# Decoder layer on one core: the output product moved ahead of u's turns, the projections to the end of the slot before

## The reference, cut to what matters

```python
x = _layernorm(x + self_attention(x))          # softmax(q k^T / sqrt(8)) v, then wo, with biases
x = _layernorm(x + cross_attention(ctx, x))    # k and v from ctx, q from x
x = _layernorm(x + ffn(x))                     # qlinear -> gelu -> qlinear
```

## Time and profile before

| what | us |
|---|---|
| median of 3 runs (lowest, highest) | 355.75 (355.57, 357.69) |
| the profiled execution's own time | 355.31 |
| its span in the profile | 353.5 |
| DVE, PE, ACT, POOL busy | 314.0, 265.0, 252.5, 187.0 |

### The profile page before, as it was taken

One profiled execution on the slowest core, in us unless ns is written; L12 is line 12 of the kernel. 1 busy time (PEld: TensorE's weight loads), 2 busy tenths in 40 slices (PEclk: granted clock), 3 DMA queues, 4 the chain that ended last, 5 costly groups with the idle time before them and its releaser, 6 DMA issues.

```text
span 353.5 us, 13237 instructions
## 1 busy us (share of the span) xinstructions
PE 265.0 (75%) x4897; PEld 171.0 (48%) x4899; DVE 314.0 (89%) x720; ACT 252.5 (71%) x502; POOL 187.0 (53%) x382
## 2 busy tenths in 40 slices
PE   3678887989989999999899988898883365102980
PEld 2446564656656666666665655555551122001660
DVE  5756799989999999999999999999889599997894
ACT  2135877988889888888888887887762599605855
POOL 6234869656675666657675667665222006400275
PEclk9999999999999999999999999999995578755797
DMA  1352323233332332323323242332000000000034
GB/s 52 89 159 69 99 80 88 63 108 90 97 107 74 107 104 84 101 84 102 106 83 107 79 124 84 96 94 71 5 3 0 0 0 0 0 0 3 1 90 149
DMA packets 48998, 25.19 MB, mean 71 GB/s; under 512 B 6440, under 2 KB 48808, under 8 KB 48936
## 3 DMA queue, kind: packets, MB, share of 16 engines
q1 hardware_dynamic: 46936, 23.76, 23.4%
q10 hardware_dynamic: 2000, 0.59, 0.7%
HBM read 9.39 MB, written 2.10 MB: 32 GB/s over the span
## 4 chain that ended last, share of the span: by engine, by line
DVE 32%; PE 30%; POOL 14%; issue 13%; DMA 4%; ACT 3%; SPq 2%; ACTq 0%; POOLq 0%; DVEq 0%; another core or an unknown queue 0%
DVE neg_max L850 14%; PE ps L1083 8%; PE ps L1109 7%; DVE h_ext L957 5%; DVE h_ext L958 5%; DMA arena_h<-parts_sk 4%; POOL rstd L531 3%; PE ps L1167 2%; PE ps L1156 2%; SPq L399 2%; PE ps L1124 2%; PE ps L1144 2%; PE ps L1131 2%; PE ps L1251 1%; POOL o_root L598 1%
## 5 line engine op out<-in xcount | busy, mean ns | idle before, releaser
L850 DVE TENSOR_REDUCE neg_max<-ps 128x8 f32<-128x1024 f32 x128 | 157.2, 1228 | 18.5 <-PE ps L1083 16.0
L652 ACT ACTIVATE probs<-ps 128x1024 f32<-128x1024 f32 x64 | 65.6, 1025 | 19.7 <-PE ps L1090 18.2
L1083 PE MATMUL ps<-arena_h 31*128 31x128 f16 x1024 | 52.8, 221 | 27.3 <-DVE neg_max L850 17.9
L663 ACT ACTIVATE probs<-ps 128x1024 f32<-128x1024 f32 x64 | 65.7, 1026 | 8.5 <-PE ps L1090 8.5
L1083 PEld LDWEIGHTS ps<-arena_h 31*128 31x128 f16 x1024 | 31.0, 94 | 59.9 <-DVE neg_max L850 35.6
L1090 PE MATMUL ps<-arena_h 32*128 32x128 f16 x1024 | 51.7, 219 | 0.6 <-ACT probs L652 0.5
L528 POOL TENSOR_TENSOR var_eps<-mean_var,eps_col 128x1 f32<-128x1 f32 x64 | 12.2, 191 | 73.4 <-DVE mean_var L833 73.4
L1109 PE MATMUL ps<-probs,arena_q 128*32 128x128 f32 x1024 | 42.1, 283 | 0.9 <-issue 0.9
L1109 PE MATMUL ps<-probs,arena_h 128*32 128x128 f32 x1024 | 41.6, 281 | 0.2 <-ACT probs L652 0.2
L531 POOL TENSOR_TENSOR rstd<-var_eps,minus_half 128x1 f32<-128x1 f32 x64 | 35.2, 550 | 5.0
L1090 PEld LDWEIGHTS ps<-arena_h 32*128 32x128 f16 x1024 | 29.6, 93 | 1.6 <-ACT probs L663 0.5
(11 more groups left out here) (155 smaller groups left out, 626.4 us busy)
## 6 DMA issues: line engine op xcount, KB each, us to landing
arena_h<-parts_sq SPq DMA_DIRECT2D x48, 64.0 KB, 2.0
arena_h<-parts_ck SPq DMA_DIRECT2D x48, 64.0 KB, 2.1
arena_h<-parts_cq SPq DMA_DIRECT2D x48, 64.0 KB, 2.0
arena_h<-parts_sk SPq DMA_DIRECT2D x45, 64.0 KB, 2.0
xT_in<-in_xT_dram SPq DMA_DIRECT2D x16, 128.0 KB, 2.6
xN_in<-in_xN_dram SPq DMA_DIRECT2D x16, 128.0 KB, 2.7
cT_in<-in_cT_dram SPq DMA_DIRECT2D x16, 128.0 KB, 2.4
cN_in<-in_cN_dram SPq DMA_DIRECT2D x16, 128.0 KB, 2.6
```

What stands on the lines that cost most here:

```text
L652: act.activation(probs[1][:, :], ps_s2, ACT.Exp, scale=SCALE).then_inc(ex, 1)
L663: act.activation(probs[0][:, :], ps_s2, ACT.Exp, scale=SCALE).then_inc(ex, 1)
L850: dve.tensor_reduce(neg_max[b.par][:, HH * half:HH * half + HH], ps_s1.rearrange("p (h k) -> p h k", h=HH), AXX, ALU.max, negate=True).the ...
L1083: ins = pe.matmul(ps_s1[:, at:at + S], q[r:r + MAX_AT, j, :], kk[r:r + MAX_AT, j, :], start=True, stop=True, skip_group_check=True)
```

## The change

What it does:
- The output product (L1191 before, L1194 after) goes from behind product(1) to mid-slot: behind the turn of the maxima and ahead of u's two turns, and it writes a quarter of bank 5 (ps_t), u's bank. Bank 7 holds projections alone (ps_p).
- projections(k + 1) is issued at the end of slot k, behind the slot's last turns and ahead of the next slot's scores(0). It waits there for its input's load and for the evacuation of the projection before it.
- Each name's parts get a second buffer, so a split waits for the stack DMAs of two pairs before. The two stacks of a pair count on one semaphore, so PE waits for one in place of two.
- Waits that others cover are left out, on PE, ACT and DVE.

The diff, cut to its core:

```diff
+
+    found = (q_pair(k), k_pair(k), S_FIRST.get(k + V_AT), C_FIRST.get(k + CK_AT))
+    return next((i for i in found if i is not None), None)
...
-        parts = {n: sb(f"parts_{n}", [128, 2, PAIR], F16) for n in NAMES}
+        parts = {n: [sb(f"parts_{n}{i}", [128, 2, PAIR], F16) for i in range(2)] for n in NAMES}
...
-        ps_o = bank(7)
+        ps_o = ps_t[:, 2 * S:3 * S]
+        ps_p = bank(7)
...
-            if i > 0:
-
-                eng.wait_ge(s_stack[name][(i - 1) % RING], landed(i - 1, RING, 16 * NTERM))
+            if i > 1:
+
+                eng.wait_ge(*stacks_landed(name, i - 2))
...
                         if half == 0 and b.half == 0:
-                            for n in (b.q, b.k):
-                                pe.wait_ge(s_stack[n][b.ring], landed(b.pair, RING, 16 * NTERM))
+                            pe.wait_ge(*stacks_landed(b.q, b.pair))
...
-                def projections():
+                def projections(k):
+
                     q, kk, vv, ck = q_pair(k), k_pair(k), S_FIRST.get(k + V_AT), C_FIRST.get(k + CK_AT)
-                    if not q is kk is vv is ck is None:
-                        need(pe, yy, tasks_to(k - 4))
+                    if projections_at(k) is not None:
+                        past_q, past_k = q_pair(k - 1), k_pair(k - 1)
+                        if past_k is not None:
+                            pe.wait_ge(eqk, 2 * past_k + 2)
+                        elif past_q is not None:
+                            pe.wait_ge(eqk, 2 * past_q + 1)
+                        for first, at, n in ((S_FIRST, V_AT, evv), (C_FIRST, CK_AT, eck)):
+                            i = first.get(k - 1 + at)
+                            if i is not None:
+                                pe.wait_ge(n, i + 1)
                     if q is not None:
...
                         pe.wait_ge(s_xT[q % LOADS], landed(q, LOADS))
-                        need(pe, evv, q)
...
                 if nxt is not None:
 
-                    pe.wait_ge(masks, 1)
-                    pe.wait_ge(mx, 2 * nxt.pos + 2)
-                    need(pe, mte, nxt.pos)
-                    need(pe, tae, tasks_to(k - 3))
-                    need(pe, txe, s_to(k - 7))
+                    if nxt.pos == 0:
+                        pe.wait_ge(masks, 1)
+                    if b is None:
+
+                        pe.wait_ge(mx, 2 * nxt.pos + 2)
+                    if task(k - 3) is None:
+
+                        need(pe, mte, nxt.pos)
+                    last_read_of_turns()
                     pe.transpose(ps_x[0:H, S:2 * S], neg_max[nxt.par][:, :], ident[:, :]).then_inc(mt, 1)
+                if w is not None and w.pos == 1:
+                    pe.wait_ge(w_step, 2)
+                if x is not None:
+                    if nxt is None:
+
+                        pe.wait_ge(tae, x.pos + 1)
+                    need(pe, yy, x.pos)
+                    pe.matmul(ps_o, attT[:, :], (wo_self if x.kind == "S" else wo_cross)[:, :],
+                              start=True, stop=True, skip_group_check=True).then_inc(oo, 1)
                 if w is not None:
...
-                if k >= LEAD_SLOTS:
-                    projections()
-
+                if k == LEAD_SLOTS:
+                    projections(k)
                 scores(1)
                 product(1)
...
-                if x is not None:
-                    pe.wait_ge(tae, x.pos + 1)
-                    need(pe, yy, x.pos)
...
-                    pe.matmul(ps_o[:, 0:D], attT[:, :], (wo_self if x.kind == "S" else wo_cross)[:, :],
-                              start=True, stop=True, skip_group_check=True).then_inc(oo, 1)
...
                     pe.transpose(ps_x[:, 2 * S:3 * S], x1_all[:, v.m, :], ident[:, :]).then_inc(tx, 1)
+                if k >= LEAD_SLOTS:
+                    projections(k + 1)
```

More of the change, by code:

```diff
@@ L274, in decoder_layer @@
         s_cN = [sem(f"cN_landed{i}") for i in range(LOADS)]
-        s_stack = {n: [sem(f"stack_{n}{i}_landed") for i in range(RING)] for n in NAMES}
+        s_stacks = {kind: [sem(f"stacks_{name}{i}_landed") for i in range(RING)] for kind, name in (("S", "self"), ("C", "cross"))}
         s_maxrow = [sem(f"max_row_landed{i}") for i in range(2)]
@@ L399, in fill @@
                     sp.dma_start(stack[name][i % RING][t::ROW_STEP, :, :],
-                                 parts[name][:, part, :]).then_inc(s_stack[name][i % RING], 16)
+                                 parts[name][i % 2][:, part, :]).then_inc(stacks_landed(name, i)[0], 16)
             def ring_free(pos, i):
@@ L618, in evacuations @@
                             need(act, split_done[name], i)
-                            act.activation(full[:, :], ps_o[:, j * PAIR:(j + 1) * PAIR], ACT.Identity,
+                            act.activation(full[:, :], ps_p[:, j * PAIR:(j + 1) * PAIR], ACT.Identity,
                                            bias=bqk_sb[:, j:j + 1]).then_inc(eqk, 1)
@@ L640, in evacuations @@
                                 act.dma_start(stack["sk"][0][t::ROW_STEP, :, :],
-                                              parts["sk"][:, part, :]).then_inc(s_stack["sk"][0], 16)
+                                              parts["sk"][0][:, part, :]).then_inc(stacks_landed("sk", 0)[0], 16)
                     i = C_FIRST.get(k + CK_AT)
@@ L881, in slot @@
                 if x is not None:
-                    dve.wait_ge(oo, x.pos + 1)
+                    if w is None:
+                        dve.wait_ge(oo, x.pos + 1)
                     if x.kind == "S":
-                        dve.wait_ge(xb, x.pair + 1)
-                        dst, own, residual = y_sb[x.place][:, :], ps_o[:, 0:D], x_bias[x.ring][:, x.half, :]
-                    else:
-                        dve.wait_ge(xn, S_POS[x.m] + 1)
-                        dst, own, residual = (by_group(y_sb[x.place][:, :]), by_group(ps_o[:, 0:D]),
+                        if x.half == 0:
+                            dve.wait_ge(xb, x.pair + 1)
+                        dst, own, residual = y_sb[x.place][:, :], ps_o, x_bias[x.ring][:, x.half, :]
+                    else:
+                        dst, own, residual = (by_group(y_sb[x.place][:, :]), by_group(ps_o),
                                               in_groups(x1_all[:, x.m, :]))
@@ L1122, in projections @@
                         pe.wait_ge(s_xT[q % LOADS], landed(q, LOADS))
-                        need(pe, evv, q)
-                        last = pe.matmul(ps_o[:, 0:PAIR], wq_g[:, :], xT_in[q % LOADS][:, :], start=True, stop=True,
+                        last = pe.matmul(ps_p[:, 0:PAIR], wq_g[:, :], xT_in[q % LOADS][:, :], start=True, stop=True,
                                          skip_group_check=True)
@@ L1128, in projections @@
                     if kk is not None:
-                        if q != kk:
-                            pe.wait_ge(eqk, 2 * kk + 1)
-                        pe.matmul(ps_o[:, PAIR:2 * PAIR], wk_g[:, :], xT_in[kk % LOADS][:, :], start=True, stop=True,
+                        pe.matmul(ps_p[:, PAIR:2 * PAIR], wk_g[:, :], xT_in[kk % LOADS][:, :], start=True, stop=True,
                                   skip_group_check=True).then_inc(pqk, 2 if q == kk else 1)
@@ L1135, in projections @@
                             pe.wait_ge(w_v, 16)
-                        pe.wait_ge(eqk, 2 * vv + 2)
                         for half in range(2):
-                            last = pe.matmul(ps_o[:, half * D:(half + 1) * D], xT_in[vv % LOADS][:, half * S:(half + 1) * S],
+                            last = pe.matmul(ps_p[:, half * D:(half + 1) * D], xT_in[vv % LOADS][:, half * S:(half + 1) * S],
                                              wv_sb[:, :], start=True, stop=True, skip_group_check=True)
@@ L1142, in projections, with last_read_of_turns @@
                         pe.wait_ge(s_cT[ck % LOADS], landed(ck, LOADS))
-                        pe.wait_ge(folded, 1)
-                        pe.matmul(ps_o[:, 0:PAIR], g_cross[:, :], cT_in[ck % LOADS][:, :], start=True, stop=True,
+                        if ck == 0:
+                            pe.wait_ge(folded, 1)
+                        pe.matmul(ps_p[:, 0:PAIR], g_cross[:, :], cT_in[ck % LOADS][:, :], start=True, stop=True,
                                   skip_group_check=True).then_inc(pck, 1)
+                def last_read_of_turns():
+                    if task(k - 7) is not None and task(k - 7).kind == "S":
+                        pe.wait_ge(txe, s_to(k - 7))
+                    else:
+                        need(pe, tae, tasks_to(k - 3))
                 scores(0)
```

49 lines of the change are left out of this document (18 added, 31 removed).

## The result

| | before | after |
|---|---|---|
| median | 355.69 us (4 runs, 355.57 to 357.69) | 359.77 us (4 runs, 359.30 to 361.25) |
| profiled execution | 355.31 (span 353.5) | 359.85 (span 358.1) |

The ratio is 1.0108, 95% interval 1.0062 to 1.0154. So the changed kernel is 1.1% slower, where 361.4 was predicted (range 352.5 to 365.5). Each line of the kernel before has moved: L850 is now L859, L860 is L869, L869 is L878, L890 is L902, L1083 is L1094, L1124 is L1145, L1167 is L1205, L1191 is L1194, L376 is L387.

What follows compares the result with a forecast made beforehand. DVE was taken as nearly the bound, with PE adding small delays per slot pair. Late loads (+5.6, +0.95, +1.6) less gains (1.1, 0.2, 0.4, 0.8) gave +5.65: 361.4 us as a median, range 352.5 to 365.5.

Steps and rivals of the forecast that it cites:

- Part 6: q projection, now at slot end, waits for its late xT load: +0.7 us per four slots, eight times, +5.6 us.
- Part 3: Even slots, one stack wait for two: PE starts 0.15 us after the maximum, gain 0.10 per even slot.
- Part 1: Projections leave mid-slot, so m1, the slot's second maximum, starts 0.05 us earlier.
- Parts 2 and 5: Mid-slot, slack absorbs r_sum's 0.08 us delay; at slot end, the projection fits with 0.06 to spare: nothing each.
- rival C: DVE's slack between r_sum and m1 isn't there: +3.4 us after overlap with the load's wait, 364.8; chance 0.12.
- Part 7: Two xT loads ahead of the eight also land late: +0.95 us at slot 8, +1.6 at slot 12.
- Part 9: Tail, slot 62: output product is ready before att, so DVE's y wait goes: -0.8 us.
- Rival D: PE idles one to two us at ten places and its clock falls: 10 x 0.9, about 370 us; chance 0.03.

Runs made afterwards that it cites:

- The two experiments on the load: xT load of pairs 6 to 15 issued one slot earlier: in the changed kernel 347.47 us (ratio 0.9823), in the kernel before 353.95 us (1.0009).
- the two kernels with held loads: Changed kernel, all loads early but four held back: 360.55 us (1.0193); the same with unread products ahead of the held q projections: 358.31 us (1.0094).

## Why the prediction was right, point by point

- **Part 6, the late load** (forecast +5.6, measured +4.64 in the same stretch). Held in every step: the issue at m0 + 4.1, no move in SyncE's queue, PE's wait 1.8 sooner, scores behind it. A cycle grew by 0.58, not 0.7: the eight loads landed 2.53 after issue on average where I took 2.6, and were issued 4.3 behind the m0, so that the 0.1 added for an earlier m0 did not appear. The 0.58 is what is left of the stall after the gains; against the version with all loads early each late load cost 1.08. The trace of before has the loads landing 0.8 to 1.7 ahead of their q projection in these eight slots, and 0.16 ahead in slot 12. The two experiments on the load prove the cause from both sides, and the one with q alone in the middle shows that k, v and ck were not involved.
- **Part 3, the waits** (0.10 forecast per even slot; measured 0.15). The gap went from 0.25 to 0.10, where I had taken the middle of 0.05 and 0.25. What counts is what stands between the last semaphore to come and the matmul: with two wait instructions from there on the gap was 0.25, with one 0.10, and with the maximum's wait written first, so that the matmul holds it, 0.05.
- **Part 1** (0.04 to 0.05 per maximum): m0 to m1 is 1.73 against 1.78. A pair takes 6.96; forecast 7.02.
- **Parts 2 and 5, which I took at nothing each**, were right for the change as a whole and wrong as separate terms. r_sum does start 0.07 later behind m0 (1.21 against 1.14) and the slack in front of m1 takes it up, so rival C fell. But that there is room rests on both moves together:

| output product | projections | cycle | ratio |
|---|---|---|---|
| behind product(1) | middle | 14.24 | 0.9930 |
| ahead of u's turns | middle | 15.02 | 1.0158 |
| behind product(1) | end of slot | 14.67 | 1.0135 |
| ahead of u's turns | end of slot, load early | 13.94 | 0.9823 |

  (All four have the single stack wait; the first is the kernel before with that alone, and the third has the load early as well.) Either move alone costs 0.4 to 0.8 a cycle; the two together gain 0.3. Each fills the room that the other one empties.
- **Part 7, slots 8 and 12** (forecast +0.95 and +1.6 in what leads up to slot 14, measured +3.12 in all). Mis-sized twice, and the two errors pull apart. Slot 8's m0 came only 0.25 later, not 0.95, but the slot lasted 4.40 in place of 3.51; slot 12 came 2.63 later and lasted 4.19. The slower clock (last section) accounts for 2.8 of the 3.12: 1.6 in the two slots (4.40 + 4.19 - 2 x 3.50), and 1.2 ahead of their maxima, since from the q projection to m0 it took 1.53 and 1.78 where the eight later slots took 1.05. That leaves 0.3 for the waits less the gains between them, where the forecast had 1.95. All this compares one execution of each kernel, and the start-up alone can differ by 1.7 (last section), so the size of either error is not shown.
- **Part 9, the tail**: -0.95 against -0.8. The y wait of the earlier trace rows is gone, in every kernel with the output product ahead of u's turns and in none without.
- **Rival D** was given 3 in 100 and priced as all or nothing. It happened at two of ten places (slots 8 and 12), and cost the 2.8 us of part 7, 1.4 each where D had 0.9. What failed is the step from one row of before (2.06 us of idle time before slot 8, granted clock 1.00) to all waits of that length: one wait that did not bring the fall is no proof for the next.

The two terms that missed (part 6 too dear by 1.0, part 7 too cheap by 1.2) nearly cancel, so the sum is closer than its parts deserve: the mechanism was right, the closeness of the sum was luck. The profiled execution took 359.85 where 361.0 was forecast for it; of that 1.15, 1.05 are the last line of the table of stretches.

The Trainium skill, DMA: Bandwidth & Descriptors, section Rules for kernel authors, advises to issue early and wait late. The runs here agree: the wait moved 1.8 us forward turned a hidden load into +4.64 us in the steady stretch, and with the issue moved one slot forward the kernel is 1.8% faster than the one before.

## What to carry to other kernels

When an instruction is moved forward, list everything that it waits for, and look up when each of these was ready before the move: PE's projection moved 1.8 us and SyncE's load did not, and the load had had some 1.1 us to spare. Two moves that look like two small gains may be one: test them together and singly. And in a loop where each of two engines waits for the other, look at what stands between the last semaphore to come and the first instruction behind it: here 0.25 us in every second slot became 0.10 with one semaphore fewer, which showed in the time (0.7% in the kernel before). The last 0.05, from the order of the waits, showed in the rows and not in the time.

## What the runs showed of the hardware that was not expected

PE's clock fell in the middle of dense work behind a single wait. PE's and DVE's timelines of the changed kernel at the end of slot 11 and in slot 12, and two of its stretches:

```profile
76.18 1.19 PE L1145 MATMUL ps<-xT_in,wq_g 128*128 128x256 f32 x2 [1.68 <-DMA xT_in<-in_xT_dram]
77.30 0.28 PE L1094 MATMUL ps<-arena_h 31*128 31x128 f16 x1
```

```profile
77.96 1.22 DVE L859 TENSOR_REDUCE neg_max<-ps 128x8 f32<-128x1024 f32 x1 [2.60 <-PE ps L1094]
79.92 0.26 DVE L869 RECIPROCAL r_sum<-ps 128x16 f32<-128x16 f32 x1 [0.73 <-PE ps L1205]
```

```profile
59.00:62.00 3.00, 3.00 (x38) 1.78 (x38) 1.65 (x3) 1.41 (x3) 2.33 (x7) 0.51 0.33 91
...
76.40:79.00 2.60, 2.60 (x35) 1.34 (x36) 1.04 (x1) 1.01 (x1) 1.10 (x2) 0.50 0.41 121
```

PE idled 1.68 us for the load, and worked at a granted clock of 0.50 (1.2 GHz) for some 2.6 us after it: the two passes took 1.19 where they take 0.67 at 1.00, the scores to the maximum 0.66 (77.30 to 77.96) where slot 36 has 0.45, and u's turns came so late that r_sum waited 0.73. Each such fall cost 0.7 to 1.9 us in the slot behind it, and behind a wait for xT another 0.3 to 0.7 between the q projection and that slot's m0 (1.35 to 1.79 in place of 1.05). The other eight waits for xT in the same kernel were 0.62 to 1.28 long, and the slots behind them took 3.45 or 3.46. In the twelve profiled executions PE has fifteen waits of over 1.3 us between slots 5 and 61. Behind eight of them (1.56 to 2.73 long) the granted clock of the 2.5 us that followed was 0.50 to 0.74, behind seven (1.39 to 2.64 long) it was 1.00. So in that range the length of a wait doesn't tell which it will be. The Trainium skill, TensorE: Matmul & The Clock Gate, section Loop structure matters more than you think, warns of a loop with a long DMA wait ahead of every matmul, in which PE goes cold. Here each long wait stood alone between stretches of dense work, and the rows show a fall behind about half of them, where the one row of before had spoken against it.

What stays open: what else decides whether a given wait brings the fall. And why the start-up, up to slot 14, differs by up to 1.7 us was not looked into: slot 14 is reached at 82.52 in the kernel before and at 80.81 with the early load, though their steady slots are alike, and at 79.73 and 81.35 in the two kernels with held loads, whose order is the same up to there.
